# One-hot rows by a compare of two tensors instead of a tensor and a scalar, and five more columns per chunk through PSUM

## What is computed

```python
# layer 1 ("sheaf"): one message to each end of an edge
out = x - zeros.at[src].add(msg_s) - zeros.at[dst].add(msg_d)
...
# layer 2 ("message"): the sum goes by row = src
m = silu(einsum('ei,ej,ijh->eh', x_j, edge_attr_e3nn, W_msg_tp) * norm)
agg = segment_sum(m @ W_msg_lin * norm, row, num_segments=n_nodes)
```

## Time and profile before

| | us |
|---|---|
| median of three runs | 30552.1 (30539.0 to 30570.65) |
| profiled execution, its time | 30782.5 |
| its span | 30780.8 |
| GpSimd busy | 22018.9 |
| VectorE busy | 9848.4 |
| TensorE matmul busy | 10582.4 |

### The profile page before, as it was taken

How to read it: one execution, slowest core, us unless ns; L and a number is a source line. 1 busy time by engine, 2 the same in 40 slices (tenths; PEclk the granted TensorE clock), 3 DMA queues, 4 the chain that set the end, 5 groups by cost and what they waited for, 6 DMA issues and landing times. The chain is left out here.

```text
span 30780.8 us, 180014 instructions
## 1 busy us (share of the span) xinstructions
PE 10582.4 (34%) x48414; PEld 7525.3 (24%) x48414; DVE 9848.4 (32%) x15298; ACT 1843.6 (6%) x4661; POOL 22018.9 (72%) x18448
## 2 busy tenths in 40 slices
PE   0000000100000026666566666648777766000004
PEld 0000000100000014444344444436555544000003
DVE  1333333311111113333333334324333332333331
ACT  0000000000000000000000000001111111000000
POOL 5665555477777648888888888778888882767665
PEclk9999999955555557766677776768888887555556
DMA  2111111011111112222222222223333322666664
GB/s 71 26 22 26 26 22 26 22 25 25 24 27 24 23 21 27 28 28 36 31 28 28 28 28 32 29 46 49 44 46 44 46 34 83 183 186 184 187 190 124
DMA packets 2135524, 1675.46 MB, mean 54 GB/s; under 512 B 959162, under 2 KB 1929348, under 8 KB 2117460
## 3 DMA queue, kind: packets, MB, share of 16 engines
q0 software_dynamic: 1151008, 593.44, 15.0%
q10 hardware_dynamic: 818050, 577.62, 6.0%
q1 hardware_dynamic: 165554, 493.75, 4.6%
HBM read 971.46 MB, written 692.02 MB: 54 GB/s over the span
## 5 line engine op out<-in xcount | busy, mean ns | idle before, releaser
L1169 POOL DMA_INDIRECT acc<-column_sums,sum_rows x4625 | 8063.9, 1744 | 1515.4 <-issue 1367.9
L717 POOL DMA_INDIRECT gathered<-gat_table,src_index x6250 | 6372.1, 1020 | 3069.2 <-issue 2060.3
L1384 POOL DMA_INDIRECT gathered<-sheaf_table,src_index x3125 | 3342.3, 1070 | 1169.2 <-issue 873.4
L2070 POOL DMA_INDIRECT gathered<-message_table,src_index x3125 | 3104.0, 993 | 1319.7 <-issue 1092.3
L1111 PE MATMUL node_sums<-placed_row,lane_values 128*128 128x392 f32 x9496 | 3545.5, 519 | 33.1 <-DVE placed_row L1100 32.0
L565 PE MATMUL transposed<-ident,last_rows 128*128 128x128 f32 (+3 forms) x5 | 2.2, 442 | 9065.0 <-DVE sums L597 9065.0
L565 PEld LDWEIGHTS transposed<-ident,last_rows 128*128 128x128 f32 (+3 forms) x5 | 0.7, 148 | 9066.7 <-DVE sums L597 9066.7
L1111 PEld LDWEIGHTS node_sums<-placed_row,lane_values 128*128 128x128 f32 x9496 | 1822.5, 199 | 1221.1 <-issue 160.3
L818 PE MATMUL histogram<-high_onehot,low_onehot 128*128 128x98 bf16 x3125 | 368.2, 279 | 4940.9 <-DVE high_onehot L746 2910.3
L2090 DVE SCALAR_TENSOR_TENSOR gathered<-gathered,same 128x256 f32<-128x256 f32 x3000 | 1459.0, 486 | 1850.1 <-issue 1319.8
L744 DVE TENSOR_TENSOR low_onehot<-iota_bf,src_low 128x640 bf16<-128x640 bf16 x625 | 515.2, 824 | 3165.6 <-remote 2268.6
(11 more groups left out here) (391 smaller groups left out, 16099.0 us busy)
## 6 DMA issues: line engine op xcount, KB each, us to landing
message_rows<-gathered ACTq DMA_DIRECT2D x250, 1600.0 KB
src_rows<-src_rows SPq DMA_DIRECT2D x225, 640.0 KB
src_rows<-src_rows SPq DMA_DIRECT2D x150, 960.0 KB
gathered<-gat_table,src_index POOLq DMA_INDIRECT x6250
gat_rows<-scanned ACTq DMA_DIRECT2D x25, 3375.0 KB
acc<-column_sums,sum_rows POOLq DMA_INDIRECT x4625
gat_rows<-scanned ACTq DMA_DIRECT2D x25, 2125.0 KB
start_values<-starts SPq DMA_DIRECT2D x50, 1062.5 KB
```

The costliest lines, as they stand in the source:

```text
L717: g.indirect_dma_start(G[b][:, j, :], None, tab, bass.IndirectOffsetOnAxis(ap=IX[b][:, j:j + 1], axis=0)).then_inc(s_g[b], 16)
L1169: g.indirect_dma_start(self.acc[i], bass.IndirectOffsetOnAxis(ap=o.IXS[b][:, j:j + 1], axis=0), o.SV[b][:, j, :], None, compute_op=ALU.add ...
L1384: g.indirect_dma_start(G[b][:, j, :], None, self.tab17, bass.IndirectOffsetOnAxis(ap=IX[b][:, j:j + 1], axis=0)).then_inc(s_g[b], 16)
L2070: g.indirect_dma_start(G[b][:, j, :], None, self.qtab, bass.IndirectOffsetOnAxis(ap=IX[b][:, j:j + 1], axis=0)).then_inc(s_g[b], 16)
```

## The change

The one-hot is made by the same comparison, but its second operand is no longer the scalar of each partition. It is a tensor operand that repeats that one element 1568 times. And in each of the two stages five more of the 125 columns go by PSUM and five fewer by GpSimd.

```diff
-MT2 = 30
-MT = 35
+MT2 = 35
+MT = 40
...
-        v.tensor_scalar(o.OW[r], o.IO[:], o.LO[b][:, i:i + 1], None, ALU.is_equal).then_inc(o.s_mv, 1)
+        v.tensor_tensor(o.OW[r], o.IO[:], bcast(o.LO[b][:, i:i + 1], [P, Q8]), ALU.is_equal).then_inc(o.s_mv, 1)
```

## The result

| | before | changed |
|---|---|---|
| median, us | 30554.2 (30539.0 to 30570.7, 4 runs) | 30877.7 (30868.8 to 30894.2, 4 runs) |
| profiled execution's span, us | 30780.8 | 30892.4 |

The ratio is 1.0106, with a 95% interval of 1.0089 to 1.0124: +323 us, where the forecast was +229 (30780 us). The interval lies wholly above 1. First the page, as in the earlier trace rows.

What follows compares the result with a forecast made beforehand. The prediction took GpSimd's queue of indirect DMAs to bound both stages. Sheaf +124, final scatters -15 and message +120 us summed to +229 us, 30780 us against the median of 30552; range 30300 to 31050 us.

Steps and rivals of the forecast that it cites:

- The bound: Sheaf and message stages: GpSimd's queue sets the pace; VectorE and TensorE have 71 and 48 us a chunk to spare.
- The duration: New one-hot on VectorE: 1568 elements take 1.79 us, against 1.04 us for the present one undisturbed.
- What catches, and when it lets go: GpSimd DMAs starting inside certain VectorE instructions wait for their end, then finish 0.82 us (gather) or 1.43 us (scatter) later.
- The late catch: Old one-hot also delays a scatter started 0.96 us ahead of it; the new one should lose this.
- The price, sheaf stage: Sheaf stage: 0.90 us per new one-hot against 0.61 before; net +5.4 us a chunk, bounds +0.2 and +12.2.
- 12.6 us for other instructions: Sheaf stage: share of the 33.9 us DMA excess a chunk put to an addition, equalities, lane values and others.
- The walk: Sheaf stage: following successive DMAs through one-hots 2.63 us apart gives 0.77 to 1.07 us lost per one-hot.
- The price, message stage: Message stage: outer, equality, one-hot trains give +18 us a chunk, taken as +14; net +5, bounds +2 and +12.
- Rival A: Both stages: the new one-hot catches nothing, 29410 us; chance 0.13.
- Rival B: Both stages: a catch costs no more than now, 30215 us; chance 0.09, including what lies between it and no change.
- Rival C: Both stages: catches at the lower bounds, so no change in time; chance 0.08.
- Rival D: The compute chain of TensorE and VectorE becomes the bound, 30900 us or more; chance 0.02.

Runs made afterwards that it cites:

- one_port: Changed kernel, but the one-hot again compares a tensor with a scalar, reading seven gapped rows at single pace: 29651.9 us, ratio 0.9629.
- halves: Changed kernel with each one-hot split into two instructions of 784 elements: 30379.7 us, ratio 0.9874.
- op_only: Kernel before with only the two-tensor one-hot, columns left at 35 and 30: 31470.2 us, ratio 1.0216.
- cols_only: Kernel before with only the five extra PSUM columns per chunk in each stage, one-hot still scalar: 30302.5 us, ratio 0.9851.

## Why the prediction came out right, point by point

**The bound.** Right. GpSimd's queue set the pace before and after (waits of 70 and 48 us a chunk remain), and the chains of the other engines stayed hidden. The columns alone gave -1.5%, and not the 13 us more a chunk that they would cost in the open.

**The duration.** 1.79 us forecast from another instruction of the setup, 1.78 to 1.79 measured.

**What catches, and when it lets go.** Right, and shown by one_port and halves. A DMA that starts in one of the changed one-hots ends 0.81 to 0.91 us (gather) or 1.42 to 1.51 us (scatter) behind it, in all 761 cases of the sheaf window that start more than 0.12 us before its end. The late catch that I saw at the old one-hot: the changed kernel's has none. In its sheaf stage, 12000 to 19000 us, 110 scatters had a one-hot begin inside them and no other VectorE instruction beside them, and none ran longer than its undisturbed time by more than 0.08 us. In the kernel before, 34 of 114 such scatters ran over by 0.15 us or more.

**The price, sheaf stage.** The net is right (the step rose by 5.5 us, forecast 5.4), but in part by luck. The excess is 85 x 0.351 + 125 x 0.156 = 49.3 us a chunk; less 12.6 that is 0.92 us a one-hot, where I took 0.90. But the 12.6 us for other instructions was an estimate, and one_port measures 17.5. The estimate left out the scans (L1503, L1568), which hold DMAs too, for 1.6 us a chunk there, a copy (L1508), and many excesses under 0.1 us each, 3.8 us together. With 17.5 the changed one-hot costs 0.80 us and the old one (33.9 - 17.5)/35 = 0.47 instead of 0.61. The steps say the same: the changed kernel's is 30.5 us above one_port's, 0.76 us for each of 40. Both prices were too high by about 0.1, and that cancels in the difference. The walk's bounds were 0.77 and 1.07, and op_only at 1.07 stands on the upper one. My walk put gathers and scatters at even shares, and the counts above are far from even in both kernels.

**The price, message stage.** This is the term that was mis-sized. The excess is 90 x 0.421 = 37.9 us a chunk, so the one-hots added 20.5 us to the 17.4 of before, where I took 14 with bounds of 11 and 22. My walk through a train had given 18, and I discounted it because GpSimd would leave trains in step. No discount was due: in 21000 to 24900 us, 544 of 670 one-hots hold a scatter, for 1.19 us each. Less the 9.3 us of the five columns that is 11.2 us a chunk; the step rose by 10.2 us, not 5. At 24 chunks that is 125 us, more than the 94 us by which the whole forecast fell short.

**Rival A** (nothing is caught, 29410 us) describes one_port, whose one-hot has no second stream: -1133 us, where A's sum was -1144. It did not describe the changed kernel: one element repeated 1568 times catches like any other tensor. The inference of the Trainium skill that I cited, that `tensor_tensor` doesn't stall such DMAs, disagrees with this trace too. **Rival B** (a catch no dearer than now) fell: at 40 and 35 columns the operation costs 1.0106 - 0.9851 = 2.6% of before, about 780 us. Its forecast of 0.989 is nearly what halves gave (0.987), by another way than B's. **Rival C** of the prediction (no change) is out too: the ratio's interval starts at 1.0089. **Rival D** did not occur.

**The sum.** The change is two edits of opposite sign: the columns -1.5%, the operation +2.6% beside them (+2.2% alone). With one_port's 17.5 and 6.9 us for the others, the same one-hot costs GpSimd 1.07 and 0.68 us in the two stages of op_only, and 0.80 and 0.89 in those of the changed kernel. In the sheaf stage the counts show what differs, mostly gathers held in the one and mostly scatters in the other. Open is why the queues fall so: eight gathers a turn instead of seven do not decide it, since cols_only, also with eight, holds 299 gathers and 159 scatters where the changed kernel holds 181 and 577. The phase between the queues is only argued.

## What to carry to other kernels

Where GpSimd issues indirect DMAs back to back and is the bound, read the excess of their mean over their minimum (the median had risen too in the changed kernel), and look at what VectorE runs when a long one starts; in this kernel each VectorE instruction with two SBUF tensors, and each one-hot at double pace, could cost that queue up to about its own length. What helped was neither the faster form nor a second tensor, but a single SBUF source at single pace (here by a gap in the rows: 1.845 us instead of 1.04, and yet 2.7% faster with the columns of before, 3.7% with five more) or, failing that, shorter pieces. Two edits made together should be timed apart: here the useful one was hidden under the harmful one.

## What I had not expected of the hardware

A scatter that started 0.06 us behind the start of `outer` (21113.92 and 21113.86, in the timeline of one_port above) was not let in at the seam but held until the equality behind it ended (21115.28), and ended 1.43 us later, at 21116.71. So a seam isn't always open. In one_port, 20300 to 23700 us, it is shut for 50 of the 167 scatters that start in an `outer` with an equality right behind it, and all 50 start 0.05 to 0.07 us behind the start of `outer`. Why is open.

Three series of runs had the kernel before at 30554, 30785 and 28918 us. The last two were on two chips; for the first the record names none. Compare such times within a series only.
